# Second stage of a vision tower block: new orders of the steps on TensorE, DVE, ACT and POOL, with attention products and scores of neighbouring groups side by side

## The reference, cut to what matters

```python
def _mha(x, w, b, ow, ob):
    L, N, _ = x.shape                       # 64, 196, 256
    qkv = x @ w.T + b
    q, k, v = jnp.split(qkv, 3, axis=-1)
    rh = lambda t: t.reshape(L, N, H, HD).transpose(1, 2, 0, 3)
    q, k, v = (rh(q), rh(k), rh(v))
    scores = jnp.einsum('nhld,nhmd->nhlm', q, k) / np.float32(np.sqrt(HD))
    attn = jax.nn.softmax(scores, axis=-1)
    o = jnp.einsum('nhlm,nhmd->nhld', attn, v).transpose(2, 0, 1, 3).reshape(L, N, D)
    return o @ ow.T + ob
...
y1 = _ln(x + _mha(x, ...), ln1_g, ln1_b)
# 8 experts: the top expert by softmax(y1 @ wg); a token beyond an expert's 1568 places is dropped
y2 = _ln(y1 + _moe(y1, wg, w1, b1, w2, b2), ln2_g, ln2_b)
```

## Time and profile before

| what | value |
|---|---|
| median of 3 executions | 1284.75 us (1284.18 to 1289.72) |
| the profiled execution | 1285.87 us, its span 1284.0 us |
| TensorE products busy | 1183.7 us, 92% of the span |
| DVE, POOL, ACT busy | 1010.5, 857.0, 720.8 us (79%, 67%, 56%) |
| mean granted TensorE clock | 0.972 of full |
| second stage | about 560 us to 1078.9 us from the span's start |

### The profile page before, as it was taken

How to read it: one execution, slowest core, us unless ns; L and a number is a source line. 1 busy time by engine, 2 the same in 40 slices (tenths; PEclk the granted TensorE clock), 3 DMA queues, 4 the chain that set the end, 5 groups by cost and what they waited for, 6 DMA issues and landing times. The chain is left out here.

```text
span 1284.0 us, 37111 instructions
## 1 busy us (share of the span) xinstructions
PE 1183.7 (92%) x11134; PEld 1086.1 (85%) x11135; DVE 1010.5 (79%) x2957; ACT 720.8 (56%) x1518; POOL 857.0 (67%) x1159
## 2 busy tenths in 40 slices
PE   1999999999999999749999999999999984999994
PEld 1999999999999999749999999999999973666662
DVE  4688888888888888705778877877788776699997
ACT  3455566566565655415555555555555540678885
POOL 1566666666666666373777777777777773378887
PEclk9999999999999999978999999999999996999997
DMA  7435555545454542211333333333233325788882
GB/s 221 165 126 157 173 155 177 164 146 172 141 184 149 179 148 90 91 42 39 113 104 110 107 107 102 110 105 110 98 111 107 110 92 157 207 236 241 238 235 93
DMA packets 97304, 180.11 MB, mean 140 GB/s; under 512 B 12319, under 2 KB 62753, under 8 KB 96226
## 3 DMA queue, kind: packets, MB, share of 16 engines
q1 hardware_dynamic: 82500, 138.66, 36.0%
q0 software_dynamic: 13312, 39.75, 8.3%
q10 hardware_dynamic: 1440, 1.07, 0.3%
HBM read 112.69 MB, written 67.80 MB: 141 GB/s over the span
## 5 line engine op out<-in xcount | busy, mean ns | idle before, releaser
L528 POOL TENSOR_TENSOR xl<-xf,xh 128x512 fp32r<-128x512 f32 x141 | 183.8, 1332 | 178.0 <-ACT xh L447 178.0
L311 PE MATMUL ps_h<-wh,xh 128*128 128x256 f32 x588 | 166.3, 283 | 4.9 <-DVE xl L669 4.9
L311 PE MATMUL ps_h<-wh,xl 128*128 128x256 f32 x588 | 166.1, 282 | 0.0
L311 PE MATMUL ps_h<-wl,xh 128*128 128x256 f32 x588 | 165.3, 281 | 0.0
L1061 POOL DMA_INDIRECT bins<-rows,slot_i x98 | 109.8, 1120 | 72.8 <-DVE rows L1172 54.0
L1462 POOL DMA_INDIRECT out<-res,c_idx x106 | 123.8, 1168 | 43.3 <-issue 21.4
L947 ACT ACTIVATE q<-b,cols_c 128x256 f32<-128x256 f32 x98 | 41.1, 471 | 158.8 <-PE ps_v L1291 155.1
L311 PE MATMUL b<-x2h,wh 128*128 128x256 f32 x392 | 120.6, 308 | 2.8 <-DVE x2l L1078 2.8
L1610 PE MATMUL c_ps_y<-w,yt 128*128 x424 | 117.9, 401 | 3.3 <-ACT yt L1409 1.7
L311 PEld LDWEIGHTS ps_h<-wh,xh 128*128 128x128 f32 x588 | 111.4, 189 | 5.7 <-DVE xl L669 5.7
L311 PEld LDWEIGHTS ps_h<-wh,xl 128*128 128x128 f32 x588 | 111.4, 190 | 0.0
(11 more groups left out here) (282 smaller groups left out, 4258.0 us busy)
## 6 DMA issues: line engine op xcount, KB each, us to landing
xf<-xt SPq DMA_DIRECT2D x49, 768.0 KB, 5.4
row<-bins SPq DMA_DIRECT2D x106, 257.5 KB
h_dram<-h1b SPq DMA_DIRECT2D x49, 256.0 KB, 5.4
x_dram<-x2o SPq DMA_DIRECT2D x49, 256.0 KB, 5.6
x<-x_dram SPq DMA_DIRECT2D x98, 128.0 KB, 2.8
rows<-h_dram SPq DMA_DIRECT2D x98, 128.0 KB
w1s<-w1t SPq DMA_DIRECT2D x8, 1024.0 KB, 6.8
w2s<-w SPq DMA_DIRECT2D x8, 516.0 KB, 5.9
```

The lines of the kernel that those rows point to most:

```text
L311: last = nc.tensor.matmul(out_ps, a, b, start=(i == 0), stop=(i == len(terms) - 1))
L528: last = nc.gpsimd.tensor_tensor(xl[:, p, part], xf[:, p, part], xh[:, p, part].bitcast(F32), ALU.subtract)
```

## The change

Only the order of the pieces in `step` and some lags change, on four engines; no piece is added, dropped or rewritten. In TensorE's table nearly all lags grow by one and `turn_x` stands last: it transposes the x of the group whose queries, keys and values follow in the next step. Where `queries`, `attend`, `rank` and `scores` stand relative to each other is new. On POOL `y1`, `count` and `send` get lag 4 instead of 3, so there is one step more. On DVE `scaled`, `gate_sum`, `place`, `expert` and `gates` change places, on ACT `z_norm`, `v_out`, `xg_out`, `k_out` and `o_hi`.

```diff
 # ScalarE
 def step(k):
-    for m, stage in ((k.back(2), v_out), (k.back(2), xg_out), (k.back(5), e_log),
-                     (k.back(2), lambda m: qk_out(m, "k_ps", kk, FT, "k_out")),
-                     (k.back(1), lambda m: qk_out(m, "q_ps", q, 0, "q_out")), (k.back(3), o_hi),
-                     (k.back(2), exps), (k.back(4), z_norm), (k, x_hi), (k.back(2), et_out)):
+    for m, stage in ((k.back(2), lambda m: qk_out(m, "k_ps", kk, FT, "k_out")), (k.back(3), o_hi),
+                     (k.back(1), lambda m: qk_out(m, "q_ps", q, 0, "q_out")), (k.back(2), exps),
+                     (k.back(5), e_log), (k, x_hi), (k.back(1), xg_out), (k.back(2), et_out),
+                     (k.back(4), z_norm), (k.back(1), v_out)):
 # GpSimd
 def step(k):
-    for m, stage in ((k.back(3), y1), (k.back(1), add_const), (k, add_bias), (k.back(3), count),
-                     (k.back(2), rstd), (k.back(2), centre), (k.back(3), send)):
+    for m, stage in ((k.back(1), add_const), (k.back(4), y1), (k.back(4), count), (k, add_bias),
+                     (k.back(2), rstd), (k.back(2), centre), (k.back(4), send)):
...
-run(pool, step, 0, NG + 3, 8, 48)
+run(pool, step, 0, NG + 4, 8, 48)
 # VectorE
 def step(k):
-    for m, stage in ((k.back(5), gates), (k.back(3), o_lo), (k.back(4), logits), (k.back(4), top_logit),
-                     (k.back(4), expert), (k.back(4), scaled), (k, x_lo), (k.back(3), residual),
-                     (k.back(3), mean), (k.back(3), gate_sum), (k.back(2), o_norm), (k.back(4), place),
-                     (k.back(1), softmax), (k.back(3), shift)):
+    for m, stage in ((k.back(3), o_norm), (k.back(4), gate_sum), (k.back(2), softmax), (k.back(3), o_lo),
+                     (k.back(4), logits), (k.back(5), scaled), (k.back(4), top_logit), (k.back(4), shift),
+                     (k.back(5), place), (k, x_lo), (k.back(5), gates), (k.back(4), expert),
+                     (k.back(3), residual), (k.back(3), mean)):
 # TensorE
 def step(k):
-    for m, stage in ((k.back(1), values), (k, turn_x), (k.back(2), turn_e), (k.back(3), project),
-                     (k.back(2), attend), (k, queries), (k.back(4), rank), (k.back(1), scores),
-                     (k.back(2), turn_o), (k, keys)):
+    for m, stage in ((k.back(3), turn_e), (k.back(4), project), (k.back(1), queries), (k.back(3), attend),
+                     (k.back(2), scores), (k.back(3), turn_o), (k.back(1), keys), (k.back(1), values),
+                     (k.back(5), rank), (k, turn_x)):
...
-run(pe, step, 0, NG + 4, 8, 48)
+run(pe, step, 0, NG + 5, 8, 48)
```

## The result

The changed kernel took 1334.97 us (median of 4, 1333.59 to 1337.06), the kernel before beside it 1285.48 us: ratio 1.0388, 95% interval 1.037 to 1.0406. The forecast of 1283 us and its range to 1293 were wrong; it is slower by 49.5 us. The profiled execution has a span of 1331.8 us against 1284.0, 47.8 us more. By the timelines 44 us of them lie in the steady part of the second stage (from the first x_hi to the last attend), and 6.2 in its end; its start is 2.1 us shorter, the third stage 0.4.

The account below looks back on a forecast made before the run. TensorE was taken as the bound. Its step falling from 9.88 to 9.72 us over some 46 steps gives -7.4 us, the tail +5.4, together -2.0: from 1284.75 to 1282.8, rounded to 1283 us, range 1274 to 1293.

Parts of the forecast that it names:

- TensorE's step by itself: TensorE's step of one group in the second stage: 9.72 us against 9.88, with turn o at 6.13.
- the register gap: On TensorE, 0.19 us of sequencer work on waits against registers, expected to fall between attend and scores.
- the faster rival: TensorE's gaps go and no path replaces them: step 9.58 us, tail 4.1, total 1275 us; chance 0.25.
- DVE alone: DVE's path from x_lo at 1.27 us through six small operations and z to the reciprocal: turn o at 6.01 us.
- The loop: The second stage's loop of steps 8 to 47, taken as eight steps per turn.
- Times of x_hi and pos taken over as they were: Starts after turn x read from the old trace and used in the sums, such as et_out at 1.59 us.
- The tail: The second stage's end, with one more POOL round and a wait for place: +5.4 us, between 3 and 7.
- The slower rival: z_norm sets the step if et_out starts at 1.68 us or later: step 9.95, total 1293.4 us; chance 0.20.

Follow-up runs that it names:

- e10: The changed kernel with POOL's y1 behind count instead of ahead of it, on chip 9: 1304.31 us, ratio 1.0137 to the kernel before.
- e16: The changed kernel with POOL's y1 moved to just ahead of send, on chip 6: 1310.91 us, ratio 1.0163 to the kernel before.
- e13: The changed kernel again, nothing edited, on chip 6: 1339.31 us, ratio 1.0385 to the kernel before.
- e9: The changed kernel again, nothing edited, on chip 9: 1313.93 us, ratio 1.022 to the kernel before.
- e7: The kernel before with all 40 steps of the loop written out, on chip 5: 1283.16 us, ratio 0.9939 to the kernel before.
- e8: The kernel before with TensorE's order queries, attend, scores, rank, and DVE's softmax ahead of place, on chip 5: 1287.37 us, ratio 0.9965.
- e6: The changed kernel with y1 behind count and all 40 loop steps written out, on chip 5: 1309.74 us, ratio 1.0139 to the kernel before.
- e3: The changed kernel with ten steps instead of two per turn of the second stage's loop, on chip 13: 1321.51 us, ratio 1.0288.

## Why the prediction was wrong

TensorE's new order does what was hoped. What failed is the forecast of when DVE and ACT get their work done beside POOL and the loop's edge, as the terms show one by one.

- **TensorE's step by itself (size near, in part by luck).** In e10's short steps, where neither edge nor late start touches it, the step is 9.69 us against the 9.72 forecast, attend is at 3.89 (3.86), turn o at 6.17 (6.13), rank to turn x without a gap (0.10 taken). But turn o there waits for an o that comes late behind the held L1153, and the register gap that was to fall between attend and scores did not come. Where nothing holds DVE, TensorE doesn't wait, and turn o is at 6.07 and the step 9.60. So it is in 13 steps of e16, one of which starts at 841.01, and in the recorded trace in the step from 605.84 on, where POOL's first DMA comes only at 613.79 (6.06 and 9.58). By itself the change was worth nearly 0.3 us a step, as the faster rival has it. First e10, turn x at 782.62, then e16:

```profile
788.79 0.66 PE L1220 MATMUL ps_o<-ident,o 128*128 128x128 f32 x4 [0.21 <-DVE o L1101]
```

```profile
844.90 1.15 PE L1318 MATMUL ps_o<-va,et 64*64 64x65 f32 x32
845.88 1.10 PE L1291 MATMUL ps_v<-k,q 64*64 64x64 f32 x32
847.08 0.66 PE L1220 MATMUL ps_o<-ident,o 128*128 128x128 f32 x4
```

- **"DVE alone" (failed).** This term took x_lo at 1.27 and the small operations "at about 0.2 each". The small operations came out near that (1.15 us for six, 824.81 to 825.96), but x_lo started at 2.80 (824.20 - 821.40). The term counted DVE's work and never asked what POOL does at the same moment. `place` had moved to just ahead of x_lo, and POOL's `y1` to the same microsecond. The mean of L1180 went from 0.187 to 1.204 us. The Trainium skill, SBUF — State Buffer, Who interferes with whom, says that a VectorE operation with two SBUF inputs contends with a GpSimd operation that reads SBUF, and that the port pair they share is an exclusive lock. The traces agree: all 44 ended with `y1`, and operations with a PSUM input kept their 0.69 us. It should have been weighed and was not.
- **The loop (failed).** With two steps per turn and `o_norm` first in DVE's order, the back edge stands on the path from z to turn o. The forecast read the loop as longer and priced its edge at nothing: 0.47 us in every second step.
- **Times of x_hi and pos taken over as they were (failed).** x_hi's 0.64 and et_out's 1.59, with its lateness of 0.35, were used as if they belonged to the instructions. They hung on where POOL's second DMA lies. The change moved that DMA from 0.8 to 0.9 us behind turn x to 0.3 us ahead of it up to 0.1 behind, and x_hi and pos then start late in the recorded trace and on three of the five chips.
- **The sum.** From 10.87 (e13) to 10.30 (e9) the late starts take 0.57, with the locks that they bring; to 10.13 (e10) `y1`'s place 0.17; to 9.69 the long steps' surplus 0.44, half of 0.88, of which 0.47 is the edge and 0.37 a later z behind the held L1153. Together 1.18, against 1.17 that the recorded step is above the forecast (10.89 to 9.72). That the two agree proves little: the parts are differences down to 9.69, which lies beside the forecast's 9.72 partly by luck, as said. Times 46 steps that is 54 us, where the steady part was 44 longer than before and 7.4 shorter was forecast, 51 in all. The parts come from different chips, so as an estimate their sizes are good to some 0.05.
- **The tail (right).** From the last attend to the close 32.1 us (1095.02 to 1127.13) against 25.87, +6.2 for the +5.4 forecast. Its parts come near too: from the last dz to the end of the last count 5.4 us more (5.3 forecast), from the last mean to dz 0.7 less (1.2), from the last attend to the last mean 1.6 more (1.3).
- **The slower rival (sign right, mechanism wrong).** Its condition, et_out at 1.68 or later, came true (2.02), but z never waited for z_norm: DVE was idle ahead of no z of that part. In the step shown z_norm ends at 824.99 and z starts at 825.96, right behind DVE's small operations, which stood behind the held one and x_lo.

## What to carry to other kernels

When operations are moved on DVE or POOL, set the two timelines side by side and look at each DVE operation with two SBUF inputs that now falls beside a long POOL operation like `y1`, which reads SBUF: here a tiny one cost as much as what was left of POOL's. Ask at which instruction a loop's back edge stands, and whether another engine waits for it there. A start that the trace shows late without a reason is not a property of the instruction; find what it follows before it is used in a sum.

## What the runs showed of the hardware that was not expected

- The same kernel, changed by nothing, had a ratio to before of 1.022 on one chip and 1.0385 on another, intervals far apart; before itself was within 0.6% over all five and the recorded result (medians 1285.5 to 1292.5). What makes the late starts come isn't known, nor whether it is the chip or the hour of the run, since the two were not varied apart. e7 and e8 on chip 5 hardly show them, since little there waits for TensorE at the wrong moment (in e7 et_out does, in about every second step).
- The late starts sit at 0.64 to 0.79 and at 1.34 to 1.57 us after the start of the second of two indirect DMAs; in seven traces of the changed order with late starts no x_hi or pos lies between, and four x_hi lie up to 0.3 us later. They were seen on DVE and ACT, for waits on TensorE. Why is open; taking the DMAs out was not tried, because the third stage reads what they write.
- In e9 L1180's row begins (764.31) 0.46 us ahead of `y1`'s (764.77), and still it ends with it, although it needs 0.18 and had the time. In the same trace the L1180 that begin 0.77 to 0.86 us ahead of `y1` take 0.19 to 0.28, and those that begin up to 0.51 ahead are held. Both kinds begin beside the second DMA, and so do e6's, 0.17 us long, so it is not the DMA that holds them. The same section of the Trainium skill says that issue order decides who blocks; by the starts of these rows it is the other way, and whether a row's start is the moment of issue the traces don't tell.
- A loop body of ten steps has a costlier back edge (6 to 7 us in e3) than one of two (0.47 on DVE's path in e10).
